# Recurrence and routed experts on one core: fewer units beside the recurrence, a second set of PSUM banks, input roots on VectorE, columns in step order

## The reference

```python
# x: 32 sequences x 256 steps x 128 features, fp32
xn   = layernorm(x, ln_w, ln_b)
u    = xn @ Ws.T + bs + xn @ Wi.T + bi            # 16 states
h_t  = tanh(h_{t-1} @ A.T + u_t)                  # scan over 256 steps
x1   = layernorm(x + (H @ Wo.T + bo) * sigmoid(xn @ Wg.T + bg) + x)
rw   = the 2 best of 8 experts by softmax(x1 @ gate_w.T) + gate_b, with their scores
expert(v, w) = silu((v @ w1 + b1) * (v @ w3 + b3)) @ w2 + b2      # 128 -> 176 -> 128
out  = layernorm(x1 + sum over experts(rw * expert(x1)) + shared_expert(x1))
```

## Time and profile before

| | us |
|---|---|
| median of 3 runs | 517.06 |
| the profiled execution's own time | 517.55 |
| its span, first to last instruction | 515.8 |
| TensorE matmul busy | 451.1 (87%) |
| VectorE busy | 347.0 (67%) |
| ScalarE busy | 336.7 (65%) |
| GpSimd busy | 302.0 (59%) |

### The profile page before, as it was taken

How to read it: one execution, slowest core, us unless ns; L and a number is a source line. 1 busy time by engine, 2 the same in 40 slices (tenths; PEclk the granted TensorE clock), 3 DMA queues, 4 the chain that set the end, 5 groups by cost and what they waited for, 6 DMA issues and landing times.

```text
span 515.8 us, 11180 instructions
## 1 busy us (share of the span) xinstructions
PE 451.1 (87%) x2842; PEld 353.6 (69%) x2842; DVE 347.0 (67%) x1562; ACT 336.7 (65%) x870; POOL 302.0 (59%) x331
## 2 busy tenths in 40 slices
PE   5879999999999988877898996899999998988691
PEld 3546766666666665666897875788888887777350
DVE  5454589898888989665757782345544568778772
ACT  3645777777777775464575764557677777777454
POOL 4100003777776775575677777777666577777232
PEclk9978999999999999799998998889999999999886
DMA  3663112333333222596465675567666588882472
GB/s 111 132 230 113 54 37 84 97 95 99 93 93 95 77 80 74 151 259 193 135 177 145 182 204 165 159 197 215 208 182 197 176 268 251 285 283 84 163 245 102
DMA packets 58228, 79.81 MB, mean 155 GB/s; under 512 B 11182, under 2 KB 37803, under 8 KB 58166
## 3 DMA queue, kind: packets, MB, share of 16 engines
q1 hardware_dynamic: 49516, 62.17, 41.7%
q0 software_dynamic: 8640, 16.93, 9.5%
q10 hardware_dynamic: 10, 0.00, 0.0%
HBM read 47.85 MB, written 25.84 MB: 143 GB/s over the span
## 4 chain that ended last, share of the span: by engine, by line
PE 48%; DVE 20%; issue 10%; POOL 9%; ACT 8%; SPq 2%; DMA 2%; ACTq 0%; DVEq 0%; POOLq 0%
PE py L1292 7%; PE p L1275 6%; PE py L1293 5%; PE pu L1347 5%; PE p L1280 5%; PE ph L1285 5%; POOL ys L585 4%; POOL xs L578 4%; PE pt L1429 2%; DVE z L1083 2%; PE pm L1406 2%; ACT hT L659 2%; DVE z L1078 2%; PE pu L1234 2%; ACT t3b L643 1%
## 5 line engine op out<-in xcount | busy, mean ns | idle before, releaser
L585 POOL DMA_INDIRECT ys<-yp,xp x142 | 145.0, 1021 | 58.6 <-issue 36.0
L578 POOL DMA_INDIRECT xs<-x,place_i x128 | 124.7, 974 | 58.9 <-issue 22.7
L659 ACT ACTIVATE hT<-pu,bu 16x32 f32<-16x32 f32 x256 | 78.7, 308 | 61.3 <-PE pu L1347 56.2
L650 ACT ACTIVATE hid<-z 128x512 f32<-128x512 f32 x103 | 64.7, 628 | 65.8 <-DVE z L1083 65.2
L1347 PEld LDWEIGHTS pu<-hT,aT 128*66 128x66 f32 x512 | 54.4, 141 | 58.0 <-ACT hT L659 52.9
L1347 PE MATMUL pu<-hT,aT 128*66 128x32 f32 x512 | 78.6, 241 | 11.9 <-ACT hT L659 11.7
L1078 DVE SCALAR_TENSOR_TENSOR z<-p,wp,t3a 128x256 f32<-128x256 f32 x71 | 34.3, 483 | 61.1 <-ACT t3a L638 54.5
L1292 PE MATMUL py<-wp,hid 128*128 128x128 f32 x284 | 59.2, 290 | 12.4 <-DVE yp L1104 9.7
L1292 PEld LDWEIGHTS py<-wp,hid 128*128 128x128 f32 x284 | 45.0, 192 | 27.9 <-DVE yp L1104 19.5
L1293 PE MATMUL py<-wp,hid 128*128 128x128 f32 x284 | 55.4, 277 | 0.0
L566 POOL TENSOR_TENSOR rstd_in<-ve_in,neghalf 128x4 f32<-128x4 f32 x16 | 16.4, 1027 | 66.3 <-DVE ve_in L793 66.2
(11 more groups left out here) (272 smaller groups left out, 969.7 us busy)
## 6 DMA issues: line engine op xcount, KB each, us to landing
wp<-packed SPq DMA_DIRECT2D x71, 320.0 KB, 3.4
xp<-xs SPq DMA_DIRECT2D x71, 130.0 KB, 2.9
weights<-ys SPq DMA_DIRECT2D x16, 512.0 KB, 4.7
xt<-in_L_attn_x SPq DMA_DIRECT2D x16, 256.0 KB, 3.1
x<-x SPq DMA_DIRECT2D x16, 256.0 KB, 2.7
packed<-weights SPq DMA_DIRECT2D x1, 2560.0 KB, 8.6
ys<-yp,xp POOLq DMA_INDIRECT x142
yb<-x SPq DMA_DIRECT2D x16, 128.0 KB, 2.7
```

Of the source, the lines that this page charges most:

```text
L578: g.indirect_dma_start(out=xs[:, :], out_offset=bass.IndirectOffsetOnAxis(ap=place_i[b % NB][:, c, t * Q + q:t * Q + q + 1], axis=0), in_= ...
L585: g.indirect_dma_start(out=ys[:, :], out_offset=bass.IndirectOffsetOnAxis(ap=xp[j % NX][:, h, DEST:DEST + 1].bitcast(int32), axis=0), in_= ...
L650: nc.scalar.activation(hid[u % NH][:, :], z[u % 2][:, :], ACT.Silu).then_inc(hid_ready, 1)
L659: nc.scalar.activation(hT[k % 2][0:N, c], pu[k % 2][0:N, c], ACT.Tanh, bias=bu[:, 0:1]).then_inc(h_ready, 1)
```

## The change

Five edits come together.

1. `KEPT = 8`: only the first halves of tiles 0 to 7 stay in the recurrence. Both halves of tiles 8 to 15 go among the pages, one half after every second page (`BETWEEN = 2`), three behind. The plan then has 95 units from slot 250 on instead of 90. The last page stands in slot 341 instead of 336, page 46, behind which the first sums start, in 317 instead of 311. In 27 slots (`QUIET`: 25 where the matmuls of the halves 8 to 12 stood, and two for tile 13), TensorE issues 4 bf16 matmuls over `ones` instead. The transposed `x1` of tiles 8 to 15 is kept in `yb`, and SP's copy of the second half is made for tiles 0 to 7 alone.
2. From slot 280 to the last page every second unit uses other banks: `pu0` for `p1`, `pu1` for `p3`, `pm` for `py` (`ph` stays single). w3a, w1a and down wait for the unit before in the same bank only. Before the first of them `bank_left` waits until the last tile has done with `pu` and `pm`.
3. The roots of the input norm of tiles 4 to 15 go from GpSimd to VectorE, in the same instructions as the middle root of tile k - 4 (8 columns for 4). The input statistics stand 3 slots later.
4. `step_cols` gives step t the 32 neighbouring columns tq*128 + q*32 + sequence. `xnT_out` reads every fourth column and writes runs, `og` is written to every fourth column.
5. `last_sum`'s first wait is split, part of it moved into `bank_left`.

```diff
-    APART, FILL, AFTER, BETWEEN = 0, 0, 3, 3
+    KEPT, AFTER, BETWEEN = 8, 3, 2
+    SWITCH = 280
...
-        start = {at("shared", k): ("shared", k, 0) for k in range(TILES) if at("shared", k) < PAGES_FROM - 8}
-        kept = [("shared", k, 1) for k in range(TILES)]
...
+        start = {at("shared", k): ("shared", k, 0) for k in range(KEPT)}
+        kept = [("shared", k, 1) for k in range(KEPT)]
+        kept += [("shared", k, h) for k in range(KEPT, TILES) for h in range(HALF)]
...
+    TWO_BANKS = [u for u, unit in enumerate(UNITS) if SWITCH <= unit[0] <= UNITS[UNIT_OF_PAGE[sum(PAGES) - 1]][0]]
+    SECOND = set(TWO_BANKS[1::2])
...
+        p1s, p3s, pys = (p1, pu[0]), (p3, pu[1]), (py, pm)
...
         def step_cols(t):
             tq, q = divmod(t, Q)
-            return slice(q * P + tq, (q + 1) * P, STEPS // Q)
+            return slice(tq * P + q * B, tq * P + (q + 1) * B)
...
+        QUIET = {at("shared", k) + SPARSE[what] for k in range(KEPT, TILES) for what in ("w3a", "w1a", "wb", "down", "down_too")}
+        QUIET = {n for n in QUIET if n < PAGES_FROM}
...
-                if k is not None:
+                if k is not None and k < LEAD:
                     rsqrt("in", k)
...
-                        ins = nc.scalar.activation(xnT[k % 2][:, cols], pm[:, cols], ACT.Identity, scale=lnw, bias=lnb)
+                        ins = nc.scalar.activation(by_step(xnT[k % 2], h), by_row(pm[:, cols]), ACT.Identity, scale=lnw, bias=lnb)
...
+                two = w == "mid" and k + LEAD < TILES
+                if two:
+                    y, ve_ = (t[i][:, :, :].rearrange("p n q -> p (n q)") for t in (rstd_two, ve_two))
...
-                    nc.vector.scalar_tensor_tensor(out=og[:, :], in0=gth[k % NG][:, :], scalar=1.0, in1=pu[k % 2][:, :],
+                    nc.vector.scalar_tensor_tensor(out=by_row(og[:, :]), in0=by_step(gth[k % NG]), scalar=1.0, in1=by_step(pu[k % 2]),
...
+            def bank_left(u):
+                if u == min(SECOND):
+                    pe.wait_ge(v_ready, TILES)
+                    pe.wait_ge(lg_ready, TILES)
+                    pe.wait_ge(x1T_ready, TILES)
+                    pe.wait_ge(place_ready, len(GROUPS))
+                    pe.wait_ge(table_step, TABLE + 1)
...
-                wait(pe, t3a_ready, u)
-                nc.tensor.matmul(p3[:, 0:PAGE], w[:, W3A:W3A + P], src, start=True, stop=True).then_inc(w3_ps, 1)
+                bank_left(u)
+                wait(pe, t3a_ready, before_in_bank(u) + 1)
+                nc.tensor.matmul(of_unit(p3s, u)[:, 0:PAGE], w[:, W3A:W3A + P], src, start=True, stop=True).then_inc(w3_ps, 1)
...
-                wait(pe, evacuated, u)
+                wait(pe, evacuated, before_in_bank(u) + 1)
...
+                if n in QUIET:
+                    pe.wait_ge(za_ready, KEPT)
+                    hold_clock(4, p1)
```

More of the change, by code:

```diff
@@ L110, in lay_out_units @@
     def lay_out_units():
-        start = {at("shared", k): ("shared", k, 0) for k in range(TILES) if at("shared", k) < PAGES_FROM - 8}
-        kept = [("shared", k, 1) for k in range(TILES)]
[L113 to L116, removed]
+        start = {at("shared", k): ("shared", k, 0) for k in range(KEPT)}
+        kept = [("shared", k, 1) for k in range(KEPT)]
+        kept += [("shared", k, h) for k in range(KEPT, TILES) for h in range(HALF)]
+        among, behind = kept[:len(kept) - AFTER], kept[len(kept) - AFTER:]
         n = PAGES_FROM
@@ L260, in rnn_gate_moe_block @@
         primer = sb("primer", [P, Q])
-        root_a, root_b = ({w: sb(f"root_{c}_{w}", [P, Q]) for w in ("mid", "out")} for c in "ab")
+        root_a, root_b = ({w: sb(f"root_{c}_{w}", [P, 2 * Q]) for w in ("mid", "out")} for c in "ab")
         tri_f, tri = sb("tri_f", [P, P]), sb("tri", [P, P], bf16)
@@ L292, in rnn_gate_moe_block @@
         x1 = sb("x1", [P, NE * 2 * Q, ROW])
-        x1T = [[sb(f"x1T{h}_{i}", [D, PAGE]) for i in range(n)] for h, n in enumerate((NS, TILES))]
+        x1T = [[sb(f"x1T{h}_{i}", [D, PAGE]) for i in range(n)] for h, n in enumerate((NS, KEPT))]
         yb = [sb(f"yb{k}", [P, Q, D]) for k in range(TILES)]
@@ L298, in rnn_gate_moe_block @@
         mv = {w: [sb(f"mv_{w}{i}", [P, Q, 2]) for i in range(NORMS[w])] for w in NORMS}
-        ve = {w: [sb(f"ve_{w}{i}", [P, Q]) for i in range(NORMS[w])] for w in NORMS}
-        rstd = {w: [sb(f"rstd_{w}{i}", [P, Q]) for i in range(NORMS[w])] for w in NORMS}
+        ve_two, rstd_two = ([sb(f"{w}_two{i}", [P, 2, Q]) for i in range(2)] for w in ("ve", "rstd"))
+        ve, rstd = ({"mid": [t[:, 0, :] for t in two], "in": [t[:, 1, :] for t in two],
+                     "out": [sb(f"{w}_out{i}", [P, Q]) for i in range(NORMS["out"])]} for w, two in (("ve", ve_two), ("rstd", rstd_two)))
         shift = {w: [sb(f"shift_{w}{i}", [P, Q]) for i in range(NORMS[w])] for w in NORMS}
@@ L398, in step_cols, with by_step, by_row @@
             tq, q = divmod(t, Q)
-            return slice(q * P + tq, (q + 1) * P, STEPS // Q)
+            return slice(tq * P + q * B, tq * P + (q + 1) * B)
+        def by_step(bank, half=None):
+            cols = bank[:, :].rearrange("d (t r) -> d t r", r=P)
+            return cols if half is None else cols[:, :, half * P // 2:(half + 1) * P // 2]
+        def by_row(cols):
+            return cols.rearrange("d (r t) -> d t r", t=STEPS // Q)
         def x1_rows(k, c):
@@ L637, in third_a @@
                 act.wait_ge(w3_ps, u + 1)
-                nc.scalar.activation(t3a[u % 2][:, :], p3[:, 0:PAGE], ACT.Identity, bias=bias_of(u, 1, P)).then_inc(t3a_ready, 1)
+                nc.scalar.activation(t3a[u % 2][:, :], of_unit(p3s, u)[:, 0:PAGE], ACT.Identity, bias=bias_of(u, 1, P)).then_inc(t3a_ready, 1)
             def third_b(u):
@@ L1093, in result @@
                     qs = slice(half * HALF, (half + 1) * HALF)
-                    if half == 1 and k >= APART:
-                        v.wait_ge(half_kept[k % NE], 16 * kept_of(k))
+                    if half == 1 and k < KEPT:
+                        v.wait_ge(half_kept[k % NE], 16)
                         own = yb[k][:, qs, :]
@@ L1314, in late_bank_free, with hold_clock @@
                 wait(pe, place_ready, sum(routed("rank", b) < n for b in range(len(GROUPS))))
-            def hold_clock(times):
+            def hold_clock(times, bank=py):
                 for _ in range(times):
-                    nc.tensor.matmul(py[:, 0:PAGE], ones[:, :], ones[:, :].unsqueeze(1).to_broadcast([P, HALF, P]), start=True, stop=True)
+                    nc.tensor.matmul(bank[:, 0:PAGE], ones[:, :], ones[:, :].unsqueeze(1).to_broadcast([P, HALF, P]), start=True, stop=True)
             def last_sum(k):
```

49 lines of the change are left out of this document (29 added, 20 removed).

## The result

The changed kernel takes 531.68 us (529.26 to 534.51), the kernel before beside it 517.03; the ratio is 1.0273 [1.0238, 1.0308], so it is slower. The prediction said 513 us, 503 to 522. The profiled execution took 531.98 us, its span is 530.2 against 515.8.

What follows compares the result with a forecast made beforehand. Bound by stage: recurrence with VectorE nearly full, pages by GpSimd to about 336 us, then almost TensorE. Terms -2.6 +3.8 +2.2 -2.0 -2.0 -2.5 -0.9 = -4.0 gave 513 us; range 509 to 518, with rivals 503 to 522.

Steps and rivals of the forecast that it cites:

- Part 2: Among the expert pages: five moved halves add 10.9 us on TensorE, about 5 hidden; net +3.8, GpSimd starving +2.2.
- part 1: In the recurrence: five first halves leave, -2.6 us; idle matmuls in their slots hold the clock at cost 0.
- Part 5: Column order in the recurrence's steps: value 0, bounds -7.7 (stride saved per step) and +7 (slower `og` write).
- rival A: Strides were paid for in every recurrence step: 0.03 us x 256 = 7.7 off, 505 us; chance 0.13.
- rival D: In the recurrence, `og` slows VectorE: +7 on the forecast, 520 us; chance 0.08.
- Part 3: Second banks from slot 280: TensorE's lead -2.0, stalls in the stretch from 341.80 -2.0, beside the sums -2.5, clock -0.9.
- The clock's 0.9: Among the pages after 336 us: a shorter stall removes half of TensorE's slow spell, -0.9 us.
- Rival E: The change does not bite: single banks were never what delayed; 517 us, chance 0.05.
- Part 4: Input roots moved to VectorE in the recurrence, where GpSimd sat idle: value 0, bounds -1 and +1.
- C: Pages 24 to 41: moved halves not hidden, 10.9 us, 523; test: whether page 23's multiply waits for a DMA; chance 0.12.
- C with D: Moved halves not hidden and `og` slowing VectorE together: the only case above 527.4 us; chance 0.05.
- the signs of being wrong: A step below 0.69, `og` above 0.9 us, no scatter wait after 300 us, pages of 2.8 beside the sums.

Runs made afterwards that it cites:

- a_k13_rows: Changed kernel with second halves of tiles 8 to 12 back in the recurrence and without the column order: 513.27 us, 0.9915.
- a_k13: Changed kernel with second halves of tiles 8 to 12 back in the recurrence (KEPT 13, BETWEEN 3), all else as changed: 519.96 us, 1.0062.
- a_early3: Changed kernel with a half after every third page among the first nine pages, after every second from there: 525.44 us, 1.0185.
- b_order_m: Kernel before with the new column order, gate and output matmuls reading row by row so `og` stays in one piece: 626.42 us, 1.0044.
- b_order: Kernel before with the new column order alone, `og` written strided: 628.05 us, 1.0028.
- b_banks_roots: Kernel before with the second set of banks and the input roots on VectorE: 636.49 us, 1.0145.

## Why the prediction was wrong

By the medians the change is -4.3 (banks and roots), +6.7 (order), +11.7 (moved halves), together +14.1 of the 14.65 measured; by the ratios to the kernel before it is -4.4, +7.6 and +10.9. Each part is measured in one order of taking them away: the halves with the column order in place, the order with the halves back. The spans of the profiled executions give +0.8, +4.3 and +9.3, because that of a_k13_rows (518.36 us) is the slowest of its seven.

*What bounds the kernel now* held: the same stages, GpSimd up to page 23, then TensorE's rhythm.

*Part 2 is the step that failed*, +3.8 + 2.2, with part 1's -2.6 a net 3.4 where 11.7 came (9.3 in the traces). The release was named rightly (page 18's landing for page 23), three pages of scatters (7.8 us) do stand less ahead of it, and the five units behind it cost 11.0 us, near the 11.6 I had put. What failed is the credit of 7.8 us against them. It holds only if GpSimd starts on the pages and is fed as before. Against a_k13 it starts 2.2 us later and starves 3.0 us longer, so 2.6 us of the credit are left. Against the kernel before it starts 5.1 us later (237.00 against 231.87), for which I had no term, and starves 6.8 us longer (12.4 against 5.6), for which I had 2.2. The release then comes 4.1 us late (340.11 against 335.99) instead of 5.6 early. With 9.1 us for the five units, in which the banks' 1.6 are already taken off, that is the 13.2 us by which the last half is late. I had costed the starvation at one unit; the half in slot 252 pushed page 2 past the hold of the transposer, and a_early3 took 4.5 to 6.2 us back by moving one half. Not all of it is the half's: a_k13 without the move also starves 9.4 us.

*Part 1*, -2.6: not seen. Tiles 10 to 14 take 66.9 us in the changed kernel and 66.75 in a_k13 with the halves' work in them (143.50 to 210.25). "Cost 0" for the idle matmuls was wrong: they lengthen most tiles by two steps of 0.4 us or so, where I had weighed 0.1 in each slot. The clock did not hold as I had said either: 0.87 and 0.66 in 180 to 200 and 200 to 220 us, where it was 1.00 and 0.84. It would have been lower without them, and that was worth 6.7 us.

*Part 5*, 0: the mechanisms of both of its bounds were there at once. The step's tanh did have 0.03 us of stride, which is rival A's mechanism; I had held it for a fixed cost because the matmul row showed none. And `og` took 0.39 us more, rival D's, by the rate of `new` that I had read (0.44). They did not cancel: in two tiles the steps gain 0.78 us, and 1.07 are lost in TensorE's order of work, at og's transposes and at rank. That makes some 1.5 us over ten tiles. Most of the rest of the 4.3 us in the traces comes in tile 14 and before page 0, beside a lower clock; which of the two leads to the other is not shown. That VectorE's fullness caps the gain was in the text; that it turns the sum to +6.7 was not. ScalarE's estimate by the Trainium skill (ScalarE: Activation LUTs, What ACT_TABLE_LOAD costs) of 307 ns for 32 columns doesn't hold in one piece: the trace has 277 ns. The rule of the Trainium skill (SBUF — State Buffer, the note on SBUF cachelines), which spoke for A and D, agrees with the tanh and with `og`. Its second half, that any access in PSUM that is not contiguous slows matmuls, hardly shows in the step's matmul: the trace has 0.31 and 0.30 us.

*Part 3*, -7.4: -1.6 in the trace. The lead was over-sized (0.9 for 2.0), and the terms for the stretch (0.1 for 2.0) and the sums (0.7 for 2.5) failed: in the changed kernel pages beside the sums still take 2.80, so single banks were not what set them. The clock's 0.9 can't be told apart. Rival E's reason was nearly right there.

*Part 4*, 0: between 0 and a gain of 0.36%, not settled.

*The rivals.* C named the right loser and nearly its price (10.9 for five units), but its test, no wait for a scatter at page 23, pointed the other way: both happened, wait and loss. D's price came in full. C with D was named, at a chance of 0.05, and gives 523 + 7 = 530, 1.7 us from the measured time, but the range ended at 522. That nearness is partly luck: C's sum still has 2.6 of part 1 and 2.5 beside the sums, of which 0 and 0.7 came. Of the signs of being wrong, a step below 0.69, `og` above 0.9 and pages of 2.8 came true.

## What to carry to other kernels

When work is moved behind a stage that another engine bounds, first follow that engine's first results through the new plan: here a credit of 7.8 us shrank to 2.6, and one half in one slot before a hold cost 4.5 to 6.2 us where its own work is 2.2. Filling an emptied slot with idle matmuls is not free either: look whether the slot already holds other work. An access order is paid at both of its ends; count the long instruction where it stands in another engine's queue, not only its nanoseconds. Take the parts of a mixed change one at a time: second banks and roots alone run in 513.27 us, and the order and the halves hid that.

## What the runs showed of the hardware

- Stride on ScalarE: a tanh of 16x32 takes 308 ns with every fourth column (16 bytes) and 277 with neighbours.
- Stride on VectorE: 128x512 float32 takes 681 ns in one piece, 1076 when written at 16 bytes, 1034 when both inputs are read at 512 bytes.
- Stride on TensorE: a matmul of 256 columns, two instructions, takes 1.10 us instead of 0.68 to 0.70 when its moving operand is read at 512 bytes, at a granted clock of 1.00 (b_order_m and b_order's repeat).
- The same kernel took 517 us in some sessions and 626 to 632 in others. It isn't the chip: the one with number 14 took 629.2 us in the first session and 517.61 in the last. ScalarE's and VectorE's instructions last the same in both (the tanh 308 and 307 ns, `og` 680); TensorE's are longer (the gate's matmul 462 against 429). The stretch from 80 to 100 us with the same parts in a 626 us session (b_banks_roots) and in another (a_k13_rows), columns as in the earlier trace rows:

```profile
80.00:100.00 20.00, 18.05 (x93) 13.32 (x94) 14.00 (x65) 11.95 (x37) 9.02 (x10) 0.75 0.27 79
```
```profile
80.00:100.00 20.00, 18.95 (x130) 13.43 (x129) 17.50 (x94) 15.35 (x48) 11.90 (x13) 1.00 0.31 91
```

  It begins just behind the first scatters of input rows: these start at 83.95 us, and the step at 87.56 takes 2.21 us. Why is open.
